# Half-precision expert products, compact softmax denominators and a moved product schedule in a two-layer gated cross-attention kernel on one core

## What is computed

```python
x = x + tanh(g_xattn[0]) * L0_attention(layernorm(x), ctx)
x = x + tanh(g_ffn[0])   * L0_experts(layernorm(x))    # h = gelu(x @ w1[e] + b1[e]); y = h @ w2[e] + b2[e]; 8 experts, 128 -> 512 -> 128
x = x + tanh(g_xattn[1]) * L1_attention(layernorm(x), ctx, mask)
x = x + tanh(g_ffn[1])   * L1_experts(layernorm(x))    # 8 experts, 128 -> 64 -> 128, and a shared one
# attention: softmax(q k^T / sqrt(8)) v, heads joined, @ wo + bo
# experts: every expert is computed for every token, the gate is zero but for the top two
```

## Time and profile before

| | |
|---|---|
| median of 3 runs | 1011.62 us (1010.51 to 1013.26) |
| the profiled execution | 1013.23 us, of which span of the profile 1011.4 us |
| busy: PE, DVE, ACT, POOL | 899.4, 730.1, 588.1, 516.9 us |
| instructions | 32583 |

### The profile page before, as it was taken

One profiled execution on the slowest core, in us unless ns is written; L12 is line 12 of the kernel. 1 busy time (PEld: TensorE's weight loads), 2 busy tenths in 40 slices (PEclk: granted clock), 3 DMA queues, 4 the chain that ended last, 5 costly groups with the idle time before them and its releaser, 6 DMA issues.

```text
span 1011.4 us, 32583 instructions
## 1 busy us (share of the span) xinstructions
PE 899.4 (89%) x13088; PEld 651.2 (64%) x13088; DVE 730.1 (72%) x1576; ACT 588.1 (58%) x1077; POOL 516.9 (51%) x662
## 2 busy tenths in 40 slices
PE   3888998989899898988999999999999899999975
PEld 1355676766767676776767776666666666666754
DVE  5675876868678587786867858777787778787723
ACT  2155666575755757557475575757666575757560
POOL 5544554545445354553555456676666576662211
PEclk9978999999999999999999999999999999999995
DMA  6245432212222122222656656676766656675200
GB/s 158 77 123 150 129 112 92 80 49 73 70 84 78 51 68 72 80 79 67 119 116 127 138 96 142 137 156 127 156 148 121 140 124 143 137 137 99 55 2 19
DMA packets 103554, 104.47 MB, mean 103 GB/s; under 512 B 28442, under 2 KB 97388, under 8 KB 103404
## 3 DMA queue, kind: packets, MB, share of 16 engines
q1 hardware_dynamic: 101986, 102.07, 43.3%
q10 hardware_dynamic: 1418, 0.32, 0.2%
HBM read 35.89 MB, written 0.46 MB: 36 GB/s over the span
## 4 chain that ended last, share of the span: by engine, by line
PE 58%; DVE 25%; ACT 9%; issue 6%; DMA 1%; ACTq 1%; SPq 0%; DVEq 0%
DVE mx L1072 14%; PE pO L1208 13%; PE pMX L1229 10%; PE pST L1187 8%; PE pKV L1274 6%; PE pKV L1265 6%; PE pFH L1399 5%; PE pFY L1328 3%; ACT P L789 2%; DVE rden L1014 2%; ACT HR L798 2%; DVE HR L970 2%; ACT L789 2%; PE pFY L1332 2%; DVE ysc L1043 1%
## 5 line engine op out<-in xcount | busy, mean ns | idle before, releaser
L1072 DVE TENSOR_REDUCE mx<-pMX 112x1 f32<-112x500 f32 x768 | 487.4, 668 | 127.9 <-PE pMX L1229 125.0
L789 ACT ACTIVATE P<-pST 125x448 f32<-125x448 f32 x768 | 389.6, 542 | 277.7 <-PE pST L1187 272.4
L1229 PE MATMUL pMX<-kop,qmax 48*112 48x500 f16 (+1 forms) x768 | 284.3, 408 | 50.1 <-DVE mx L1072 37.3
L1187 PE MATMUL pST<-qexp,kop 50*128 50x112 f16 (+2 forms) x3072 | 266.7, 215 | 13.0 <-ACT P L789 7.9
L1187 PEld LDWEIGHTS pST<-qexp,kop 50*128 50x128 f16 (+2 forms) x3072 | 183.7, 100 | 78.0 <-issue 23.8
L1208 PE MATMUL pO<-P,V 125*17 125x112 f32 x6144 | 188.5, 264 | 0.0
L1229 PEld LDWEIGHTS pMX<-kop,qmax 48*112 48x112 f16 (+1 forms) x768 | 97.4, 129 | 124.0 <-DVE mx L1072 57.6
L1208 PEld LDWEIGHTS pO<-P,V 125*17 125x17 f32 x6144 | 138.1, 98 | 35.0 <-issue 18.7
L641 POOL CAST khi<-kfull 128x500 f16<-128x500 f32 x96 | 57.7, 601 | 190.1 <-ACT kfull L816 188.6
L643 POOL TENSOR_TENSOR klo<-kfull,khi 128x500 f16<-128x500 f32 x96 | 108.8, 1134 | 7.8
L732 POOL TENSOR_TENSOR Clo<-C,Chi 128x500 f16<-128x500 f32 x93 | 105.7, 1137 | 7.5
(11 more groups left out here) (151 smaller groups left out, 1106.8 us busy)
## 6 DMA issues: line engine op xcount, KB each, us to landing
C<-in_ctxT SPq DMA_DIRECT2D x31, 750.0 KB, 6.7
kop<-maskop SPq DMA_DIRECT2D x48, 437.5 KB
kop<-khi SPq DMA_DIRECT2D x192, 62.5 KB
kop<-khi SPq DMA_DIRECT2D x96, 125.0 KB
kop<-klo SPq DMA_DIRECT2D x96, 62.5 KB
kop<-klo SPq DMA_DIRECT2D x48, 125.0 KB
maskin<-in_mask SPq DMA_DIRECT2D x8, 656.2 KB, 5.5
qexp<-qmax SPq DMA_DIRECT2D x16, 182.0 KB
```

The lines of the kernel that those rows point to most:

```text
L789: nc.scalar.activation(P[0:KP, slot, h * 4 * T:(h + 1) * 4 * T], pST[0:KP, h, 0:4 * T], ACT.Exp, scale=EXP_SCALE).then_inc(exp_done, 1)
L1072: nc.vector.tensor_reduce(mx[:, s % 2, c, p:p + 1], pMX[0:T, m % 2, 0:CW], AX.X, ALU.max).then_inc(max_done, 1)
L1187: mm = nc.tensor.matmul(pST[0:keys.stop - keys.start, h, i * T:(i + 1) * T], kop[rows, b, slot, keys], qexp[rows, b, slot, :, :].rearrange ...
L1229: nc.tensor.matmul(pMX[0:T, m % 2, 0:CW], qmax[rows, b, slot, :, :].rearrange("r j q -> r (j q)"), kop[rows, b, slot, c * CW:(c + 1) * CW] ...
```

## The change

It has six parts.

- **fp16 products.** The first expert weights of layer 0 and their operand are each split into a high and a low fp16 part (`w1hi`, `w1lo`, `xfhi`, `xflo`). Each fp32 product becomes three fp16 products into the same PSUM columns. The weights arrive in the space of `HR`; ACT rounds them (8 instructions of 128x512) and GpSimd forms the rest (8 of 128x512) in steps 2 and 3. The last expert's weights are loaded in step 3. DVE makes two more 128x112 instructions after `xT`.
- **Compact denominators.** `V` gets a second column of ones (`VW` = 18), so that each head has a sum row of its own. `OM`, `rden` and `ON` shrink from 224 columns to 112. DVE forms `OM` with two instructions that depend on each other. The sum product has 112 columns, `y` has two products in place of four. The start loses the eight instructions that built `bvm`.
- **Other sub-steps.** `h6` and `h7` move from sub-steps 4 and 5 to 6 and 7. `ct` moves from the end of sub-step 0 into the middle of sub-step 1, on PE and on DVE.
- **ACT takes `y1` and `y3` out of PSUM** in steps below 32: `y1` at sub-step 11 and `y3` at sub-step 3, ahead of the exponentials there.
- **GpSimd multiplies by the gates** (two instructions of 112x512 per group, after the low parts of key chunks 0 and 1 in odd steps).
- **GpSimd updates `X`** with two instructions of 112x128, except in the last step.

```diff
-VW = PR + 1
+VW = PR + 2
@@ fh_uses, fy_uses
-        uses += [(e - 2, f"h{e}", 1) for e in range(2, 8)]
+        uses += [(k, f"h{e}", 1) for e, k in zip(range(2, 8), (0, 1, 2, 3, 6, 7))]
...
-        uses.append((0, "ct", 1))
+        uses.append((1, "ct", 1))
@@ expert_weights (SP)
-                if s in (1, 2):
-                    for e in range(4 * (s - 1), 4 * s):
-                        sp.dma_start(w1a[:, e, :], w1_0[e]).then_inc(w1_in[e // 2], 16)
+                if s in (1, 2, 3):
+                    for e in range(4 * (s - 1), min(4 * s, E0 - 1)) if s < 3 else (E0 - 1,):
+                        if e == E0 - 1:
+                            sp.wait_ge(w1_split, 1)
+                        sp.dma_start(w1raw[:, raw_columns(e)], w1_0[e]).then_inc(w1_in[e], 16)
@@ GpSimd
+            def expert_low(st, i):
+
+                if st.s in (2, 3):
+                    e = 4 * (st.s - 2) + i
+                    pool.wait_ge(w1_hi, e + 1)
+                    apart(pool)
+                    nc.gpsimd.tensor_tensor(w1lo[:, e, :], w1raw[:, raw_columns(e)], w1hi[:, e, :], ALU.subtract
+                                            ).then_inc(w1_split, 1)
...
+                def weight_products(k):
+
+                    if has_end(s) and not ends(s) and plain(s if k else s - 1):
+                        pool.wait_ge(fy_free, upto(fy_uses, s if k else s - 1, f"y{2 * k + 1}", True))
+                        apart(pool)
+                        part = ysc[:, k, :, :]
+                        link(nc.gpsimd.tensor_tensor(part, part, gate[:, 4 * k:4 * k + 4].unsqueeze(2).broadcast_to([T, 4, D]),
+                                                     ALU.mult))
...
                 low_part(st, 0)
+                expert_low(st, 0)
+                weight_products(0)
                 mask_part(st, 0)
                 low_part(st, 1)
+                expert_low(st, 1)
+                weight_products(1)
                 mask_part(st, 1)
...
+                    pool.wait_ge(ysum_done, end_count(s) + 1)
+                    apart(pool)
+                    g = 2 + layer_of(s - 4)
+                    link(nc.gpsimd.tensor_scalar(acc[:, 1, :], acc[:, 1, :], gains[0:T, g:g + 1], None, ALU.mult))
+                    pool.wait_ge(fy_free, upto(fy_uses, s, "yb", True))
+                    apart(pool)
+                    nc.gpsimd.tensor_tensor(xg((s - 5) // 2), acc[:, 1, :], acc[:, 0, :], ALU.add).then_inc(x_done, 1)
@@ ACT
+            def products_out(s, use):
+
+                k = int(use[1]) // 2
+                act.wait_ge(fy_ready, upto(fy_uses, s, use))
+                if use == "y1" and s >= 6:
+                    act.wait_ge(ysum_done, end_count(s))
+                nc.scalar.activation(ysc[:, k, :, :], pFY[0:T, 0:4 * D].rearrange("t (e d) -> t e d", e=4), ACT.Copy
+                                     ).then_inc(fy_free, 1)
...
+                    if kt == 11 and has_f(s) and plain(s):
+                        products_out(s, "y1")
+                    if kt == 3 and has_end(s) and plain(s):
+                        products_out(s, "y3")
                     exps(st, kt, 0)
...
+                    if s in (2, 3) and kt in (1, 3, 5, 7):
+                        e = 4 * (s - 2) + kt // 2
+                        act.wait_ge(w1_in[e], 16)
+                        nc.scalar.activation(w1hi[:, e, :], w1raw[:, raw_columns(e)], ACT.Copy).then_inc(w1_hi, 1)
@@ DVE
-                        nc.vector.reciprocal(rden[:, :], pFY[:, 0:2 * T]).then_inc(fy_free, 1)
+                        nc.vector.reciprocal(rden[:, :], pFY[:, 0:T]).then_inc(fy_free, 1)
...
+                            link(nc.vector.tensor_copy(xfhi[:, :], pFY[:, 0:T]))
+                            nc.vector.tensor_tensor(xflo[:, :], pFY[:, 0:T], xfhi[:, :], ALU.subtract).then_inc(fy_free, 1)
...
+                    elif use in ("y1", "y3") and plain(s - back):
+                        pass
...
-                        nc.vector.tensor_tensor(OM[:, s % 2, :], pO[:, 0:2 * T],
-                                                headmask[:, :, :, :].rearrange("p r j q -> p (r j q)"),
-                                                ALU.mult).then_inc(o_free, 1)
+                        of = pO[:, 0:2 * T].rearrange("p (r j q) -> p j r q", r=2, j=2)
+                        om = OM[:, s % 2, :].rearrange("p (r q) -> p r q", r=2)
+                        link(nc.vector.tensor_scalar(om, of[:, 0], headmask[:, 0:1], None, ALU.mult))
+                        nc.vector.scalar_tensor_tensor(out=om, in0=of[:, 1], scalar=headmask[:, 1:2], in1=om,
+                                                       op0=ALU.mult, op1=ALU.add).then_inc(o_free, 1)
@@ PE
-                        mm = nc.tensor.matmul(pFY[:, 0:2 * T], sel[:, :], OM[:, s % 2, :], start=True, stop=True)
+                        mm = nc.tensor.matmul(pFY[:, 0:T], sel[:, :], OM[:, s % 2, :], start=True, stop=True)
...
-                                    mm = nc.tensor.matmul(pFH[:, c * T:(c + 1) * T], w1a[:, e, c * 128:(c + 1) * 128],
-                                                          xnfT[:, :], start=True, stop=True)
+                                    for i, (w1, x_) in enumerate(((w1hi, xfhi), (w1hi, xflo), (w1lo, xfhi))):
+                                        mm = nc.tensor.matmul(pFH[:, c * T:(c + 1) * T], w1[:, e, c * 128:(c + 1) * 128],
+                                                              x_[:, :], start=(i == 0), stop=(i == 2))
```

103 lines of the change are left out of this document (59 added, 44 removed).

## The result

The changed kernel is **slower**: 1025.53 us median of 4 runs (1021.33 to 1029.59), against 1011.07 us for the kernel before beside it (1010.39 to 1013.26). The ratio is 1.014, with a 95% interval from 1.009 to 1.018. The forecast was 988 us (range 972 to 1006). The profiled execution took 1021.33 us, its span is 1019.2 us; it is the shortest of the four runs, 4.2 us under their median.

A forecast was written before the change was run, and what follows sets the result against it. PE was taken as nearest to a bound, with DVE on the chain where PE waits for maxima. Gains of 14.0 + 6.0 + 1.8 + 2 = 23.8 us gave 988 us against a median of 1011.62, range 972 to 1006.

The forecast's parts named there:

- End of the odd steps: Layer 0's odd steps: X leaves DVE and h0, h1 get shorter, 1.1 us gained per group (ends 0.8 and 1.4).
- GpSimd's new work: End of odd steps: GpSimd's two X instructions precede the context splitting, which has a step of slack; cost 0.
- fp16 products: Hidden products: an expert takes 0.84 us instead of 1.15, 0.31 less for each of 64, 20 us of PE.
- Even steps of layer 0: First GELU 1.05 us earlier, less 0.4 for ScalarE's y1 copy at the end, in each of eight groups.
- Middle of the odd steps: y3 leaves DVE and y halves its products: 0 in layer 0, 1.0 us in each of six layer 1 steps.
- in odd steps `y2` and `y3` add slack on PE: Move of ct to sub-step 1: the later copy and DMAs are covered by slack, cost 0 (ends 0 and 0.7 per step).
- Layer 1's even steps: Shorter rden less what OM costs: 0.3 us gained in each of six steps, 1.8 us in all.
- Tail: After the last steps: shorter rden, sum and y, less OM's cost, gain 2 us.
- The start: Steps 2 and 3: eight more instructions each on ACT and GpSimd, hidden by idle time, taken as 0; at most 9 us.
- The slower rival: PE's clock falls behind all 14 even steps, 2.5 us each: 1023 us; chance 8%.
- The signs: Right if layer 0 steps near 30.2 and 29.6 us, expert within 0.9, rden near 0.8, PE busy 35 us less.
- signs of "wrong": Scores waiting for ct's DMAs, PE waiting over 1 us for ACT, over two half-clock stretches in layer 1, or late ON.

The follow-up runs named there:

- four_and_cc_first: Kernel before with fp16 products, their new places, ScalarE's copies, X on GpSimd, and GpSimd waiting for cc: 994.2 us, ratio 0.980 to the kernel before.
- four_alone: Changed kernel without compact denominators and the move of ct, with no GpSimd wait for cc: 1007.0 us, ratio 0.994 to the kernel before.
- plus_compact: fp16_cc_first with the compact denominators added: 1006.9 us, ratio 0.996 to the kernel before.
- plus_ct: fp16_cc_first with ct moved to sub-step 1: 1004.5 us, ratio 0.993 to the kernel before.
- cc_first: Changed kernel with GpSimd waiting for VectorE's cc before splitting the context, from step 4 on: 1012.7 us, ratio 0.997 to the kernel before.
- wide_sums: Changed kernel with denominators summed over 224 columns again and OM one instruction: 1013.1 us, ratio 1.000 to the kernel before.
- ct_back: Changed kernel with ct in sub-step 0 again: 1014.5 us, ratio 1.001 to the kernel before.
- before_cc_first: Kernel before with only GpSimd's wait for cc added: 1005.6 us, ratio 0.992 to the kernel before.
- fp16_cc_first: Kernel before with fp16 hidden products, h6 and h7 at sub-steps 6 and 7, and GpSimd's wait for cc: 998.1 us, ratio 0.985.
- plus_act_copies: fp16_cc_first with ScalarE taking out y1 and y3 and GpSimd applying their gates: 995.6 us, ratio 0.984 to the kernel before.
- clean base: The kernel of fp16_cc_first, to which parts of the change were added one at a time: 998.1 us, ratio 0.985 to the kernel before.
- fill: Changed kernel with products that compute nothing added ahead of PE's waits for OM and for scores: 1015.5 us, ratio 1.003 to the kernel before.
- cc_first_fill: Changed kernel with the edits of cc_first and fill together: 1012.2 us, ratio 0.999 to the kernel before.

## Why the prediction was wrong

The budget, in per cent of the kernel before: four_and_cc_first 98.0, `cc` and DVE behind GpSimd 1.3 (four_alone), compact denominators 1.1 (plus_compact), `ct` 0.8 (plus_ct). That makes 101.2, measured 101.4; each has about 0.3 of uncertainty, so that it closes this well is in part luck. Undone in the changed kernel itself the three are 1.7, 1.4 and 1.3 (cc_first, wide_sums, ct_back), since one edit moves what the others cost. The forecast was 97.7.

The 98.0 is no proof that the gains were forecast rightly: GpSimd's wait is not part of the change and is worth 0.8 in the kernel before alone. Against that kernel with the wait (before_cc_first, 99.2) the other edits are worth 1.2%, 12 us, half of the 23.8 us forecast for the whole change, and `cc` behind GpSimd costs 0.5 more than it did. So the gains were half of what was forecast, and three costs taken at nothing or nearly so add some 24 us: `cc` 5, compact denominators 11, `ct` 8.

- **End of the odd steps: the step that failed first.** Layer 0's odd steps were to be 1.1 us shorter and are 0.4 longer at full clock. The prediction gave the removal of `X` the 1.11 us of its row, for 1.1 us per group. Its own rows held the warning: mean 802 ns for `X`, 351 for a like instruction that reads PSUM. It noted both and didn't ask what the 0.45 in between was. It was waiting for GpSimd (343 ns in before_cc_first). Moving `X` is worth 0.13 us once nothing waits, and 0.25 as the kernel stood.
- **GpSimd's new work "0".** Its slack was judged by its own deadlines. What counted was who waits beside it: DVE's `cc`, 0.36 and 0.17 us before, 0.78 and 0.51 now, and 0.43 to 1.09 in layer 1's even steps.
- **fp16 products: right.** The forecast took 0.84 us for an expert. The chain has 0.59 to 0.62 for most, 0.89 to 1.15 before. From the first start to the last end, which is what the 0.84 was, twelve take 0.75 to 0.77 us, and what they replace 1.15: 0.38 us less, with 0.31 forecast. The rule of the Trainium skill that the prediction set against it ("TensorE: Matmul & The Clock Gate", section "Back-to-back issue gap"), some 81 ns per product, an estimated 0.97 us for twelve, is not what this stream shows: 0.55 us lie between the first start and the twelfth, 50 ns per product.

```profile
381.74 0.60 PE pFH L1476 x12
...
390.63 0.59 PE pFH L1476 x12
```

- **Even steps of layer 0: the mechanism right, the size too small.** Forecast -0.65 us (1.05 less 0.4), measured -1.5: products and places 1.1 (fp16_cc_first), compact denominators 0.4 (plus_compact). The 0.4 set aside for ScalarE's copy at the end is not seen: 29.83 us with and without it (plus_act_copies).
- **Middle of the odd steps.** In layer 0 "0" was 0.3 (`OM`) and 0.4 to 0.8 (`ct`) less what `y` gave. In layer 1 the forecast of -1.0 came to nothing: `OM` +0.3 at sub-step 4, `rden` gave 0.7 at sub-step 5 and it came back at 6 (2.64 to 1.93, then 2.68 to 3.39 us), and `ct` +0.16 (ct_back; +0.5 on the clean base). `OM`'s two instructions were priced rightly (0.32 and 0.33) and `rden` too (0.85); they were taken as beside PE where they were on the path.
- **`ct`: "in odd steps `y2` and `y3` add slack on PE".** The opposite: `y2` uses the same bank and queues behind it.
- **Layer 1's even steps**, forecast -0.3, measured +0.8: `cc` 0.65 by its length (0.5 came back in cc_first), and 0.2 from `OM`.
- **Tail.** Forecast -2, measured -0.2 (54.2 to 54.0 from the last maximum but one): the clock is at its lower level for longer there, 31.3 against 28.9 us. The start is left open: steps 0 to 3 took 1.7 us more, but the other kernels' spread from 103 to 110 us, and not in order of their time at the lower clock (10 us in the shortest, 17 in the longest).
- **The slower rival** (8%) named the granted clock, and its 1023 us is near the result. It put falls behind the light end of all 14 even steps, 2.5 us each, and held against it that the fp32 products of `y0` and `y1` guard layer 0. They came in layer 0, behind that end and at the wait for `OM`, and cost some 12 us, not 35 (10.4 in the odd steps and 1.4 in step 26, with 3.6 in the kernel before; in `fill`, 11 came back). Right in kind, wrong in place, a third of the size: that its sum comes near the result is luck, since the other losses filled the place. No rival had GpSimd.
- **The signs.** An expert within 0.9 us and `rden` near 0.8 came. None of the signs of "wrong" did: PE waited for `ct`'s DMAs once (1.1 us), for ScalarE 0.8 us at most, and from step 20 on there is one fall. PE is busy 12 us less, not 35. The signs looked where the prediction had doubts, not at VectorE's small instructions.

## What to carry to other kernels

When an instruction's mean is well above that of its like, find out what it waits for before pricing its removal: if it is another engine, the next instruction inherits the wait. Price a move on GpSimd by what VectorE does beside its long instructions, not by GpSimd's idle time; one wait that orders them was worth 0.8% in the kernel before and 1.3 to 1.7% with the change. In a kernel like this one, edits that make TensorE wait a little more can cost clock (plus_compact: 2 us of steps, 11 us of time), or not (plus_act_copies), so they are priced best one by one on a base without falls.

## What the runs showed of the hardware

- A VectorE instruction of 8 columns, 0.17 us alone, took up to 1.09 us and ended within 0.03 us of a GpSimd instruction's end. Elementwise instructions from SBUF to SBUF waited (`cc`, both its forms, and `X`); the reduction to `m8` and the reductions out of PSUM beside the same `Clo` did not. The Trainium skill states this ("SBUF — State Buffer", section "Who interferes with whom"): VectorE and GpSimd share a port pair, of two instructions that need it the one that issues first has it for its whole length, and a `tensor_reduce` on trn2 never contends. The trace agrees: `cc` (start 884.73) lasts until the `Clo` that began at 884.66 ends, and `m8` is not held up. The case in which VectorE comes first was not looked at. The prediction hadn't drawn on this.
- PE is busy for 87 to 89% of the span in these kernels, and its granted clock still falls from 2.4 to 1.2 GHz, in stretches of 3.4 or 6.8 us. In layer 0's odd steps, over all the kernels, a short one cost 1.3 to 1.8 us, a long one 2.7 (once 3.1). PE's single waits shortly ahead of the changed kernel's falls were 0.92 us at most. Products that compute nothing, put into PE's waits, kept the clock up in most places (seven falls to two).
- Which steps are hit depends on edits elsewhere (cc_first_fill, ct_back): what decides it beyond PE's waits just ahead was not settled.
